# Graph attention kernel, layer 2: eight one-hot slots for four, and row gathers issued in groups of four

## What is computed

```python
xr = jnp.einsum('nd,rdf->rnf', x, W)
oi = xr[etype, dst]
oj = xr[etype, src]
alpha = jax.nn.leaky_relu(oi @ q + oj @ k, 0.2)
m = jax.ops.segment_max(alpha, dst, num_segments=n_nodes)
e = jnp.exp(alpha - m[dst])
z = jax.ops.segment_sum(e, dst, num_segments=n_nodes)
a = e / (z[dst] + 1e-16)
msg = (a[:, :, None] * oj.reshape(-1, heads, out_ch)).reshape(-1, heads * out_ch)
out = jax.ops.segment_sum(msg, dst, num_segments=n_nodes) + b
```

## Time and profile before

| | |
|---|---|
| time, median of 3 runs | 2626.19 us (2621.61 to 2630.13) |
| span of the profiled execution | 2992.0 us |
| TensorE busy | 2709.4 us, 91% |
| VectorE, ScalarE, GpSimd busy | 1043.9, 1126.5, 1726.6 us |
| DMA, mean over the span | 168 GB/s |
| layer 2's aggregation, first to last step | 655.5 us from 2327.7 to 2983.2 |

### The profile page before, as it was taken

The page is one execution under the profiler, slowest core; times in us unless marked ns, Lnnn a source line. Parts: engine busy times, 40 slices in busy tenths (PEclk is TensorE's granted clock), DMA queues, the critical chain, the costliest instruction groups (busy, mean ns, idle before and its releaser), DMA issues.

```text
span 2992.0 us, 44927 instructions
## 1 busy us (share of the span) xinstructions
PE 2709.4 (91%) x10749; PEld 1768.7 (59%) x10749; DVE 1043.9 (35%) x2056; ACT 1126.5 (38%) x3158; POOL 1726.6 (58%) x1798
## 2 busy tenths in 40 slices
PE   8879889998989999999988898899989899999998
PEld 7745455555558888888876554555545444444444
DVE  8420401122167777777776010000001222222222
ACT  2310110010138888888866000010011444555554
POOL 1356766666326666666644666666660666666665
PEclk9999999999999999999999999999999999999999
DMA  7531232222238888888863322221211888888887
GB/s 240 168 85 48 53 106 69 64 79 68 85 117 266 272 266 272 263 268 273 259 193 104 96 83 63 64 62 53 58 56 57 279 283 281 281 284 290 291 291 235
DMA packets 163296, 503.02 MB, mean 168 GB/s; under 512 B 59466, under 2 KB 59873, under 8 KB 162713
## 3 DMA queue, kind: packets, MB, share of 16 engines
q0 software_dynamic: 99824, 354.55, 37.7%
q1 hardware_dynamic: 54987, 143.82, 15.2%
q10 hardware_dynamic: 8396, 3.49, 0.5%
HBM read 414.42 MB, written 87.24 MB: 168 GB/s over the span
## 4 chain that ended last, share of the span: by engine, by line
PE 76%; another core or an unknown queue 9%; issue 7%; DVE 3%; DMA 2%; ACT 1%; DVEq 1%; ACTq 0%; POOL 0%; SPq 0%; POOLq 0%
PE banks L661 31%; PE banks L770 20%; PE banks L793 10%; PE banks L789 10%; PE banks L557 2%; PE banks L519 1%; DMA ring<-xr_table,row_idx 1%; PE banks L573 1%; DVE ring L1214 1%; ACT ring L927 1%; PE banks L544 1%; PE banks L682 0%; DVEq L1507 0%; DVE big L1452 0%
## 5 line engine op out<-in xcount | busy, mean ns | idle before, releaser
L661 PE MATMUL banks<-work 128*125 128x384 f32 x3600 | 1235.5, 501 | 107.5 <-ACT ring L927 66.4
L1172 POOL DMA_INDIRECT ring<-xr_table,row_idx x880 | 837.2, 951 | 539.9 <-issue 196.5
L661 PEld LDWEIGHTS banks<-work 128*125 128x125 f32 x3600 | 688.5, 193 | 624.7 <-issue 96.6
L1150 POOL DMA_INDIRECT big<-k_table,row_idx x830 | 798.7, 962 | 408.5 <-issue 233.3
L770 PE MATMUL banks<-ring,work 128*125 128x193 f32 x3520 | 636.6, 335 | 53.1 <-issue 36.1
L770 PEld LDWEIGHTS banks<-ring,work 128*125 128x125 f32 x3520 | 570.9, 188 | 118.9 <-issue 82.5
L927 ACT COPY ring<-banks 125x384 f32<-125x384 f32 x300 | 139.6, 480 | 1235.1 <-PE banks L661 667.5
L955 ACT ACTIVATE work<-work,wE 128x125 f32<-128x125 f32 x1760 | 552.5, 388 | 137.0 <-PE banks L770 101.3
L1512 DVE TENSOR_TENSOR big<-big,banks 125x772 f32 x440 | 421.6, 958 | 165.7 <-PE banks L770 134.9
L789 PE MATMUL banks<-ring,work 128*125 128x384 f32 x880 | 365.6, 497 | 40.8 <-issue 27.0
L793 PE MATMUL banks<-ring,work 128*125 128x386 f32 x880 | 368.9, 501 | 11.3 <-issue 11.1
(11 more groups left out here) (226 smaller groups left out, 1001.4 us busy)
## 6 DMA issues: line engine op xcount, KB each, us to landing
xr_table<-ring SPq DMA_DIRECT2D x75, 337.8 KB
xr_table<-ring SPq DMA_DIRECT2D x75, 336.9 KB
x_turned<-work SPq DMA_DIRECT2D x40, 375.0 KB, 2.6
work<-x_turned SPq DMA_DIRECT2D x40, 375.0 KB
ring<-xr_table,row_idx POOLq DMA_INDIRECT x880
work<-in_L_gnn_W SPq DMA_DIRECT2D x36, 384.0 KB, 7.3
big<-k_table,row_idx POOLq DMA_INDIRECT x830
out<-work SPq DMA_DIRECT2D x25, 336.0 KB
```

Of the source, the lines that this page charges most:

```text
L661: last = pe.matmul(bank[u % DBANKS][0:TN, 0:n_cols], xT_slot(k, TN)[:, c, :], w_cols(r, first, n_cols)[:, c, :], start=(c == 0), stop=(c = ...
L1150: nc.gpsimd.indirect_dma_start(k_at(l, st), None, ktab[l], bass.IndirectOffsetOnAxis(ap=row_idx[:, st:st + 1], axis=0)).then_inc(s["k_gath ...
L1172: nc.gpsimd.indirect_dma_start(ring[:, st % GS, 0:ROWW[l]], None, xrtab[l], bass.IndirectOffsetOnAxis(ap=row_idx[:, st:st + 1], axis=0)).t ...
```

## The change

Two lists replace two constants; their first entries leave layer 1 as it was. `HOT_SLOTS = [AHEAD, GS]` gives layer 2 eight one-hot slots in place of four (the array takes the last 1000 columns of `work` in place of the last 500, which hold nothing else at that time), and L975's wait asks for the step eight before in place of four. `BURST = [1, 4]` lets GpSimd wait only before every fourth gather of layer 2, for the `step_done` that the fourth of the group needs: before gathers st to st+3 it waits for `st + 4`, which asks for the steps up to st-5.

```diff
+    HOT_SLOTS = [AHEAD, GS]
+    BURST = [1, 4]
...
-        one_hots = [work[:, sum(WORK) - AHEAD * h * TN:].rearrange("p (s h n) -> p s h n", s=AHEAD, h=h) for h in HEADS]
+        one_hots = [work[:, sum(WORK) - n * h * TN:].rearrange("p (s h n) -> p s h n", s=n, h=h) for n, h in zip(HOT_SLOTS, HEADS)]
...
-                        pe.matmul(sums[0:TN, bass.ds(at, HALF)], one_hots[l][:, st % AHEAD, 0, :],
+                        pe.matmul(sums[0:TN, bass.ds(at, HALF)], one_hots[l][:, st % HOT_SLOTS[l], 0, :],
                                   ring[:, st % GS, 0:HALF], start=False, stop=False, skip_group_check=True)
...
-                            gate(s["step_done"], st + 1 + GS - AHEAD)
-                            nc.scalar.activation(one_hots[l][:, j % AHEAD, 0, :], gaps[:, j % AHEAD, :], ACT.Relu,
+                            gate(s["step_done"], st + 1 + GS - HOT_SLOTS[l])
+                            nc.scalar.activation(one_hots[l][:, j % HOT_SLOTS[l], 0, :], gaps[:, j % AHEAD, :], ACT.Relu,
...
                 for st in range(STEPS):
-                    pool.wait_ge(s["step_done"], st + 1)
+                    if st % BURST[l] == 0:
+                        pool.wait_ge(s["step_done"], st + BURST[l])
                     nc.gpsimd.indirect_dma_start(
```

More of the change, by code:

```diff
@@ L54, in rgat_kernel @@
     GS = 8
+    HOT_SLOTS = [AHEAD, GS]
+    BURST = [1, 4]
     KG = 11
-    assert STEPS % GS == 0 and STEPS % (2 * KG) == 0
+    assert STEPS % GS == 0 and GS % BURST[1] == 0 and STEPS % (2 * KG) == 0
     U = 5
@@ L792, in _ @@
                             tiles = tile_count(st + 1)
-                        pe.matmul(sums[0:TN, bass.ds(at + 512, ROWW[l] - HALF)], one_hots[l][:, st % AHEAD, 0, :],
+                        pe.matmul(sums[0:TN, bass.ds(at + 512, ROWW[l] - HALF)], one_hots[l][:, st % HOT_SLOTS[l], 0, :],
                                   ring[:, st % GS, HALF:ROWW[l]], start=False, stop=False, skip_group_check=True
```

## The result

The changed kernel takes **2700.27 us** (2697.33 to 2712.3) against 2628.16 us (2621.61 to 2630.14) for the kernel before, measured beside it: ratio 1.0281, 95% interval 1.0264 to 1.0298, so 72 us more. The forecast was 2651 with a range up to 2685: the sign is right, the size is nearly three times too small, and the time lies above the range.

The account below looks back on a forecast made before the run. TensorE, busy 91% of the span, was taken as the bound, with late step-done words causing most holds in layer 2's loop. Late words +15 us and tile ends +10 us on 2626 gave 2651 us, range 2608 to 2685.

Parts of the forecast that it names:

- they arrive no later than the first does: Layer 2's groups: three following gathers leave 1.25 us apart against uses 1.30 us apart, so only the first's lead matters.
- stands at every fourth step: Expected sign: TensorE's idle time before layer 2's first half step, put down to row landings, at each fourth step, mostly behind tile ends.
- the prediction's last test: Layer 2's loop: if TensorE idles evenly over all steps, the groups of gathers are not the cause.
- a margin of 0.6 us: Spare lead of a group's first gather with short delays: d + g of 4.6 us against 5.2 us, so no stall.
- g: Time from a gather's start to its first matmul in layer 2: taken as 4.4 us, between 4.17 and 10.5.
- d: Delay of the word to GpSimd that a step is done: 0.04 to 0.24 us at best, 3.0 to 3.8 at worst.
- 15 tile ends at 0.7: Store and load traffic at layer 2's tile ends delays the group behind it by 0.7 us, 15 times: +10 us.
- Profiled and unprofiled: Whole kernel: plain runs have 256 us over clean matmul time, the profiled one 622, so 0.41 of the loop's holds remain unprofiled.
- 0.4 x 110 x 0.34: Late words in 0.4 of layer 2's loop cost 0.34 us in each of 110 groups: +15 us.
- No change: Rival: long delays are the profiler's alone, groups cost only low-end tile ends; 0 to +8 us, 2626 to 2634; chance 0.25.
- Faster: Rival: one-hots hold TensorE in plain runs too and gathers still land in time; 2591 to 2608 us; chance 0.13.
- Slower by the full amount: Rival: long delays as common unprofiled, +37 us, with tile ends +54; 2663 to 2680 us; chance 0.15.

Follow-up runs that it names:

- e2: Eight one-hot slots alone, a wait before every gather as in the kernel before: 2628.69 us, ratio 1.0008 to the kernel before.
- e3: Gathers in groups of four alone, with four one-hot slots as in the kernel before: 2701.2 us, ratio 1.0289 to the kernel before.
- e4: Full change without groups, every gather waiting for step k-5 (four steps of lead): 2718.46 us, ratio 1.0345 to the kernel before.
- f1: The full change run again, on the chip of f2: 2701.75 us, ratio 1.0281 to the kernel before.
- f2: Full change without layer 2's later input loads and all stores but the last tile's: 2661.85 us, ratio 1.0114 to the kernel before.
- e1: The kernel before, unchanged, recorded once more on a usual chip: 2626.79 us, profiled span 2625.1 us.
- e5 to e8: Slow-chip runs: f2's kernel 2993.69 us; eight slots, groups of two 2989.12; ungrouped gathers, five steps' lead 3000.70; full change, tile number read before waits 3005.85.

## Why the prediction was right or wrong

**The mechanism: right in the main.** The kernel is slower because the gathers have four steps of lead in place of seven. The waits stand before L791, are put down to the ring's rows and lie mostly near tile ends; GpSimd waits once in four; the slots are worth nothing on a usual chip. e2 and e3 part the slots from the groups, and e4 parts the lead from the grouping. One step of it failed: "they arrive no later than the first does", and with it the sign that the idle time "stands at every fourth step". It stands on all four steps of a group (11, 12, 7 and 10 stalls in f1), because each of the four gathers has the short lead and any of them can land late. By the prediction's last test (idle evenly over all steps means that the groups are not the cause) one would have cleared the groups, and e3 shows that they are the cause.

**What made the size wrong: a margin of 0.6 us, and a single g.** These are the steps that failed. With d + g = 4.6 the forecast gave quiet stretches no loss at all, and tile ends +10 us. The runs show +33 us without any tile end (f2 over before, 2661.85 - 2629.11) and 40 us from the tile ends (f1 less f2).

**"g", 4.4 us: low, and taken as one number.** It was taken near the lower end of 4.17 to 10.5, and the lower end itself had been made by taking 0.56 us off the first gather. Landing alone takes 4.6 us at the median and the hand-over to TensorE 0.18, so g is 4.8; with d at 0.28 there remains 0.1 us of 5.2 in place of 0.6. And landings are spread: 159 of 406 take over 4.8 us. Whatever lands later stalls the group.

**"15 tile ends at 0.7", +10 us: the largest miss.** It measured 40 us. Three parts of the term were too small. It took 15 ends of 25, by the false share. It subtracted a margin of 0.6 us where 0.1 was left, and took the middle between nothing and the whole. And it counted idle time alone, where 11 of the 40 us are late starts. One part was too large and hid some of this: a load goes out at 6 tile ends only, so the 750 KB and their 2.1 us hold for those, and at the rate used there the 375 KB of the others are 1.1 us. The landings bear this out: 1.1 us over the quiet median beside a store, 2.8 beside both. An estimate from these, with the margin of 0.1, is 18 x 1.0 + 6 x 2.7 = 34 us for the 24 ends that f2 leaves out, near the 40 measured.

**"Profiled and unprofiled": failed.** The 366 us between the profiled execution and the runs were laid on the profiler, and a share of 0.41 of the holds was carried over to plain runs. e1 shows the profiler adding nothing, and the plain runs beside e5 to e8 show a chip on which before takes 2988 us without it: the record was that of such a chip, as far as its length and its late words tell. The share itself took work for holds: in e1 TensorE idles for only 2625.1 - 2547.5 = 77.6 us of the whole span, and not 256. The term that followed, 0.4 x 110 x 0.34 = +15 us of late words, is zero on the usual chips, where the word takes 0.24 to 0.28 us. The same mistake shows in the forecast of the loop's length in the profile, 680 to 700 us: it is 657.3, from 583.7 and not from 655.5. That the difference could lie between two chips was among none of the cases weighed.

**The rivals.** "No change" was argued from the quick word at the loop's ends; that was correct, and still the change costs 72 us, because it doesn't need a late word. "Faster" fell: the earlier trace rows had 204.3 us of ScalarE's waits, and e2 gives 1.0008. On the usual chip such waits, 234.6 us before L976 in e1, are the slack of an engine that is done early. "Slower by the full amount" had 2663 to 2680, nearer in size, from a cause (late words) that is absent. The range ended where that cause ended. The upper end of g, the 10.5 us of the earlier trace rows, was named and never used in it: a first gather that takes so long is 10.5 + 0.2 - 5.2 = 5.5 us late, at 25 tile ends 137 us, which would have put the measured time well inside the range.

**The two rules.** The estimate of 2.9 us for a gather, from the Trainium skill (DMA: Bandwidth & Descriptors, Anatomy of one DMA), was set aside for the trace's 4.17 to 4.73. The measurement decides: no gather of those 406 landed under 3.7 us. The rule of the Trainium skill (Perfetto Trace Analysis, Optimization Strategy) that a repeated gap can mean too few buffers spoke for the one-hot slots, and e2 shows no gain by them.

## What to carry to other kernels

The lead of a prefetch has to cover the slow landings, not the median: here, with a median of 4.6 us, a lead of 7.8 us still lost 11 us against one of 9.1, and every step of 1.3 us given up cost more than the one before. A wait that stands for several loads gives the first of them the lead of the last's condition, and followers that leave at the pace at which they are used have hardly more. So count lead and not waits. And when a recorded span and the runs are far apart, record the kernel again before any wait is read from it: the waits belong to that execution and may not exist in the others.

## What the runs showed of the hardware

- Of three chips one ran this kernel in 2988 us and two in 2627 to 2629, with a granted clock of 0.97 against 0.99. In the record that fits the slow one, a word from TensorE reaches others 3 to 4 us late in place of 0.24 to 0.28. Why is open, and so is whether it is the chip or its state in that session.
- A gather of 128 rows (394 KB) lands in 4.6 us at the median beside other gathers, 3.7 at least. Near a tile's end the median is 5.6 us beside a store of 375 KB and 7.3 beside store and load, and the longest is 8.5 (10.0 in e1). Beside the five loads at the loop's start (1.9 MB) e1 has landings of up to 14.0 us.
- From a landing to the matmul that waited for it pass 0.18 us.
- In the stretch shown, a restart of TensorE costs some 0.7 us beyond its wait, spread over the stalled step and the next, in which each weight load starts within 0.01 us of its matmul in place of 0.3 us ahead.
- Reading one number from memory into TensorE's registers takes 0.29 us at the median and 1.86 at most.
